# Four scatters of a half body, each waiting for the landing of the one before

## The chip, the cores and the metric

One core of a Trainium2 chip. The time is the device time of the kernel in microseconds, as a median of runs. The core has TensorE (PE), VectorE (DVE), ScalarE (ACT), GpSimd (POOL) and SyncE (SP), and 16 DMA engines that all of them share.

## What is computed

An embedding lookup with pooling: 512 examples, 32 features, each feature with a table of 12500 rows of 64 float32. For each example and feature up to 20 ids are given and a length; the rows of the first `length` ids are added.

```python
B, F, V, L, E = (512, 32, 12500, 20, 64)
emb = flat[ids + offs]                       # (B, F, L, E)
mask = (jnp.arange(L_) < lengths[..., None]).astype(emb.dtype)
pooled = jnp.einsum('bfle,bfl->bfe', emb, mask)
out = pooled.reshape(Bq, F_ * E_)
return jnp.nan_to_num(out)
```

## The kernel before

The 32 features are done in two ways side by side. M = 22 of them are *counted*: the kernel loads the whole table of a feature, builds one-hot matrices of the ids on VectorE (L740, L742), multiplies them on TensorE to counts (L515), lets ScalarE copy these to SBUF (L470), and multiplies the counts with the table (L525). Each feature is two halves of 256 examples, each half 7 chunks, so 14 stages per feature. VectorE reads the sums of a half at L778. TensorE's features run in a hardware loop, ScalarE's, VectorE's and SyncE's instructions are written out.

The other 10 features are *gathered*. They make 40 tiles of 128 bags (a bag is one example and feature). In the prologue the bags are sorted by their length through 40 scatters to DRAM (L402), so that bags of like length share a tile. Then GpSimd fetches, for tile after tile, the rows of slot l of all 128 bags with one indirect DMA (L427), as many slots as the longest bag of the tile has. `rows` has 8 buffers, one for each tile of a body; there are 5 bodies of 8 tiles. Gathers of one tile alternate between two semaphores, and each waits for the landing of the last one on its own semaphore. So about two are in flight.

VectorE adds the rows of a tile (L800, `add_rows`) at fixed places in its own program: tile t is added in stage ADDS of a feature, the first in feature 2, the last in feature 18, stage 4. It waits there for the tile's landed rows. SyncE fills the buffer with zeros and new row numbers when a tile was added. After every 4th tile VectorE cleans the 4 sums of the half body and signals `gathered_ready`. GpSimd then scatters the four sums, 64 float32 for each of 128 bags, to their places in the output (L437, `put`). All of these are issued from GpSimd's one queue, in the order of the program: in a body, the put of the first half of the body before stands ahead of tile 2, that of the second half ahead of tile 6 (`PUT_AT = 2`). The last two puts come behind all gathers.

The four scatters of a put share the semaphore `gathered_stored[x]` (x is the half). Who waits for it: VectorE ahead of the first sum of the same half one body later (L795), and GpSimd at the end. `fill_begun` is a counter that nobody waits for.

Of the kernel before, what the change touches and what calls it, by code (L numbers as in the profile page):

```python
# [36 lines left out]
SLOTS = BUFFERS // 2  # L37
PUT_AT = 2

def turn(l):  # L40
    return l % 2
# [40 lines left out]
def build_embedding_bag(nc, ids, lengths, tables, lookup_ids, lookup_lengths, lookup_place, ramps, triangle,  # L82
# [43 lines left out]
    with ExitStack() as ctx:  # L126
# [6 lines left out]
        def sem(name):  # L133
            return ctx.enter_context(nc.semaphore(name))
# [115 lines left out]
        fill_begun = sem("fill_begun")  # L250
        added = sem("added")
        gathered_ready = sem("gathered_ready")
        gathered_stored = [sem(f"gathered_stored{x}") for x in range(2)]
# [47 lines left out]
        def sorted_tile(t):  # L301

            return TILES - 1 - t // 2 if t % 2 == 0 else t // 2

        def column(t):
            return t % BUFFERS * BODIES + t // BUFFERS
# [76 lines left out]
        @block.gpsimd  # L383
        def _(pool):
            for out, pattern, base, by in (
                (value, [[1, L + 1]], 0, 0),
                (first_row, [[V, G], [0, L]], M * V, 0),
                (position, [[0, G], [1, L]], 0, 0),
                (records[:, :, L], [[P, TILES]], 0, 1),
                (lane[:], [[1, 1]], 0, 1),  # L390
            ) + tuple(
                (last_rank[:, column(k):column(k) + BODIES],
                 [[(sorted_tile(k + BUFFERS) - sorted_tile(k)) * P, BODIES]], sorted_tile(k) * P + P - 1, 0)
                for k in range(BUFFERS)
            ):
                nc.gpsimd.iota(out, pattern=pattern, base=base, channel_multiplier=by).then_inc(iotas_done, 1)
            last_row = pool.to_reg(F * V - 1)

            for k in range(BLOCKS):
                pool.wait_ge(records_ready, k + 1)  # L400
                for t in range(k * G, (k + 1) * G):
                    nc.gpsimd.indirect_dma_start(  # L402
                        out=sorted_records, out_offset=bass.IndirectOffsetOnAxis(ap=rank[:, t:t + 1], axis=0),
                        in_=records[:, t, :], in_offset=None).then_inc(records_out, 16)
            pool.wait_ge(records_out, 16 * TILES)
            for t in range(BUFFERS):
                s = sorted_tile(t)
                nc.gpsimd.dma_start(row_now[:, t, :], sorted_records[s * P:(s + 1) * P, :]).then_inc(first_records_in, 16)
            pool.wait_ge(depths_ready, 1)
            pool.wait_ge(first_records_in, 16 * BUFFERS)  # L410

            def gather(b, k):

                pool.wait_ge(buffer_ready[k], b * 32 + 16)
                pool.sem_inc(fill_begun, 1)
                n = pool.value_load(depth[0:1, bass.ds(b + column(k), 1)], min_val=2, max_val=L)
                landed = [pool.value_load(arrived[0:1, x, bass.ds(b + column(k), 1)], min_val=0, max_val=16 * L * BODIES)
                          for x in range(2)]
                with ExitStack() as deeper:
                    for l in range(L):  # L420
                        if l > 1:
                            deeper.enter_context(pool.If(n > l))
                        x = turn(l)
                        if l > 1:
                            pool.wait_ge(rows_in[k][x], landed[x] + 16 * sum(turn(i) == x for i in range(l)))
                            pool.sem_inc(fill_begun, 1)
                        nc.gpsimd.indirect_dma_start(  # L427
                            out=rows[:, k, l * E:(l + 1) * E], out_offset=None, in_=table_rows,
                            in_offset=bass.IndirectOffsetOnAxis(ap=row_now[:, k, l:l + 1], axis=0),
                            bounds_check=last_row, oob_is_err=False).then_inc(rows_in[k][x], 16)  # L430

            def put(b, x):

                pool.wait_ge(gathered_ready, b * 2 + (x + 1))
                pool.sem_inc(fill_begun, 1)
                for k in range(x * SLOTS, (x + 1) * SLOTS):
                    nc.gpsimd.indirect_dma_start(  # L437
                        out=out_gathered, out_offset=bass.IndirectOffsetOnAxis(ap=place_now[:, k:k + 1], axis=0),
                        in_=gathered[:, k * E:(k + 1) * E], in_offset=None).then_inc(gathered_stored[x], 16)

            def body(b, first):
                for k in range(BUFFERS):
                    if not first and k % SLOTS == PUT_AT:
                        put(b - 1, k // SLOTS)
                    gather(b, k)

            body(0, True)
            with pool.Fori(1, BODIES) as b:
                body(b, False)
            for x in range(2):  # L450
                put(BODIES - 1, x)
                pool.wait_ge(gathered_stored[x], 16 * SLOTS * BODIES)
# [447 lines left out]
```

## Time and profile before

| what | us |
|---|---|
| time, median of 3 runs | 1190.97 (1186.9 to 1194.51) |
| span of the profiled execution, first to last instruction | 1287.7 |
| TensorE busy in it | 1118.5 |
| VectorE busy | 992.5 |
| ScalarE busy | 827.6 |
| GpSimd busy | 547.5 |

The profiled execution was recorded by the hardware profiler and is another one than the three that were timed. Its span alone is 96.7 us longer than the median of those; its own time with what lies around the span is not given. Durations are read from it, and are compared with the timed runs where they differ.

### The profile page before, as it was taken

The numbers are of one execution on the slowest core, as the hardware profiler recorded it, in microseconds if no ns is written. First come the engines' busy times: TensorE is split into PE (matmuls) and PEld (weight loads), VectorE is DVE, ScalarE is ACT, GpSimd is POOL, SyncE is SP. The second block draws the span as 40 slices with busy tenths as digits, with TensorE's granted clock in tenths as the row PEclk, the third lists the DMA queues.
The fourth block names the chain that finished last, engine by engine and source line by source line (L and its number), as shares of the span: only waits on it lengthen the run. The fifth ranks groups of instructions, "written<-read, shape, count | busy, mean of one in ns | idle before, by whom it ended". The sixth has DMA issues, their size and how long they took to land.

```text
span 1287.7 us, 31751 instructions
## 1 busy us (share of the span) xinstructions
PE 1118.5 (87%) x10873; PEld 969.4 (75%) x10873; DVE 992.5 (77%) x2692; ACT 827.6 (64%) x1233; POOL 547.5 (43%) x519
## 2 busy tenths in 40 slices
PE   3379999896988878989979888979789999999996
PEld 1168888785876767778868767868678888888886
DVE  9657788884886867869868867969678898787881
ACT  4257787673756656757747566757557777787780
POOL 4865665556555455555565544555540101000000
PEclk9989999897999988999989989989989999999998
DMA  5324234241433333242414333242413213123120
GB/s 184 116 68 115 60 83 144 74 136 45 135 107 95 117 86 97 81 132 82 143 46 136 106 95 118 82 130 69 134 25 100 58 55 104 47 62 100 35 73 5
DMA packets 63916, 118.38 MB, mean 92 GB/s; under 512 B 30120, under 2 KB 31742, under 8 KB 63840
## 3 DMA queue, kind: packets, MB, share of 16 engines
q1 hardware_dynamic: 46608, 102.19, 25.5%
q0 software_dynamic: 16032, 15.00, 5.9%
q10 hardware_dynamic: 1200, 0.50, 0.2%
q14 instruction: 68, 0.56, 0.1%
q8 instruction: 8, 0.13, 0.0%
HBM read 87.19 MB, written 4.62 MB: 71 GB/s over the span
## 4 chain that ended last, share of the span: by engine, by line
PE 73%; DVE 10%; another core or an unknown queue 7%; ACT 7%; issue 3%; DVEq 0%; POOL 0%; POOLq 0%
PE sums L525 48%; PE pairs L515 19%; PE rest L543 6%; DVE onehot_j L742 3%; ACT counts L470 3%; ACT table L482 2%; DVE gathered L800 1%; DVE onehot_p L740 1%; ACT rest L478 1%; DVE table L751 1%; ACT table L486 0%; DVE table L759 0%; DVEq L796 0%; DVE is_nan L768 0%
## 5 line engine op out<-in xcount | busy, mean ns | idle before, releaser
L525 PE MATMUL sums<-table,counts 128*128 128x192 bf16 x8624 | 909.0, 251 | 0.8 <-issue 0.8
L470 ACT ACTIVATE counts<-pairs 128x588 int16<-128x588 f32 (+1 forms) x968 | 617.0, 650 | 368.9 <-PE pairs L515 262.7
L525 PEld LDWEIGHTS sums<-table,counts 128*128 128x128 fp8e3 x8624 | 776.3, 98 | 55.0 <-issue 0.4
L427 POOL DMA_INDIRECT rows<-tables,row_now x413 | 453.3, 1098 | 376.7 <-issue 206.1
L742 DVE TENSOR_SCALAR onehot_j<-ramp,j_of,worth 128x296 bf16<-128x296 f16 x1848 | 536.3, 353 | 0.0
L515 PE MATMUL pairs<-onehot_j,onehot_p 128*128 128x294 bf16 x1892 | 410.4, 297 | 112.8 <-ACT counts L470 67.3
L740 DVE TENSOR_TENSOR onehot_p<-ramp,p_of 128x768 bf16<-128x768 f16 x308 | 169.9, 552 | 253.7 <-PE pairs L515 172.9
L515 PEld LDWEIGHTS pairs<-onehot_j,onehot_p 128*128 128x128 bf16 x1892 | 178.2, 98 | 187.3 <-issue 107.8
L543 PE MATMUL rest<-table,minus_eye 128*128 128x448 bf16 x352 | 102.5, 373 | 38.2 <-ACT table L482 17.1
L486 ACT ACTIVATE table<-rest 128x896 f32<-128x896 f32 x88 | 80.8, 918 | 35.3 <-remote 23.6
L437 POOL DMA_INDIRECT out_gathered<-gathered,place_now x40 | 42.4, 1061 | 132.3 <-DVE gathered L771 121.0
L482 ACT ACTIVATE table<-rest 128x896 f32<-128x896 f32 x88 | 80.8, 918 | 26.1 <-remote 9.8
L800 DVE TENSOR_REDUCE gathered<-rows 128x64 f32<-128x1280 f32 x40 | 94.3, 2356 | 0.0
L478 ACT ACTIVATE rest<-table 128x896 f32<-128x896 f32 x88 | 80.7, 917 | 0.0
L751 DVE TENSOR_TENSOR table<-table 128x896 f32<-128x896 f32 x66 | 71.5, 1083 | 0.0
L759 DVE TENSOR_TENSOR table<-table 128x896 f32<-128x896 f32 x66 | 69.5, 1053 | 0.0
L543 PEld LDWEIGHTS rest<-table,minus_eye 128*128 128x128 bf16 x352 | 24.2, 98 | 58.4 <-ACT table L482 25.6
L402 POOL DMA_INDIRECT sorted_records<-records,rank x40 | 45.6, 1139 | 26.3 <-DVE records L617 14.4
L778 DVE TENSOR_REDUCE pooled<-sums 128x128 f32<-128x384 f32 x44 | 23.8, 542 | 21.3 <-PE sums L525 20.5
L728 DVE TENSOR_SCALAR onehot_j<-ramp,j_of,worth 128x296 bf16<-128x296 f16 x44 | 17.3, 392 | 0.0
L726 DVE TENSOR_SCALAR onehot_p<-ramp,p_of 128x128 bf16<-128x128 f16 x44 | 12.8, 291 | 0.0
L771 DVE COPY_PREDICATED pooled<-is_nan,zeros 128x256 f32<-128x256 uint8 x22 | 10.0, 453 | 0.8
(68 smaller groups left out, 79.8 us busy)
## 6 DMA issues: line engine op xcount, KB each, us to landing
table<-tables SPq DMA_DIRECT2D x154, 448.0 KB
rows<-zeros SPq DMA_DIRECT2D x40, 640.0 KB
rows<-tables,row_now POOLq DMA_INDIRECT x413
out_counted<-pooled SPq DMA_DIRECT2D x132, 21.0 KB
rows<-lookup_ids SPq DMA_DIRECT2D x1, 903.0 KB, 8.5
rows<-lookup_lengths SPq DMA_DIRECT2D x1, 903.0 KB, 10.2
out_counted<-pooled SPq DMA_DIRECT2D x44, 1.0 KB
sorted_records<-records,rank POOLq DMA_INDIRECT x40
```

The lines of the kernel that those rows point to most:

```text
L427: nc.gpsimd.indirect_dma_start(out=rows[:, k, l * E:(l + 1) * E], out_offset=None, in_=table_rows, in_offset=bass.IndirectOffsetOnAxis(ap= ...
L470: nc.scalar.activation(dst, src, ACT.Copy).then_inc(counts_saved, 1)
L478: nc.scalar.activation(rest[:, :, 0:CE // 2], both_halves(0, c), ACT.Copy).then_inc(chunk_copied, 1)
L482: nc.scalar.activation(both_halves(1, c), rest[:, :, 0:CE // 2], ACT.Copy).then_inc(middle_ready, 1)
L486: nc.scalar.activation(both_halves(2, c), rest[:, :, 0:CE // 2], ACT.Copy).then_inc(low_saved, 1)
L515: last = nc.tensor.matmul(pair(h, c, q)[:, x, 0:WIDE], onehot_p[:, s, k, :, side], onehot_j[:, s, i + 1, 0:WIDE], start=True, stop=True)
L525: last = nc.tensor.matmul(sums[h][:, k * PARTS * E:(k + 1) * PARTS * E], counts[h][:, j, :, k], parts[:, :, j, :, 1], start=(j == 0 and k ...
L543: last = nc.tensor.matmul(rest[:, x, 0:CE // 2], minus_eye[:], upper_halves(part)[:, half], start=False, stop=True, skip_group_check=True)
L740: nc.vector.tensor_tensor(onehot_p[:, s, 1:, :, :], ramp_twice.unsqueeze(1).to_broadcast([P, PAIRS, P, 2]), of_chunk.unsqueeze(2).to_broad ...
L742: nc.vector.tensor_scalar(onehot_j[:, s, i + 1, :], ramp[:, 2 * P:], j_of[:, n:n + 1], worth[:, 0:1], ALU.is_equal, ALU.mult).then_inc(one ...
L751: nc.vector.tensor_tensor(table[:, 1, sl], table[:, 0, sl], upper_halves(0)[:, sl], ALU.subtract).then_inc(rest_done, 1)
L800: nc.vector.tensor_reduce(out=gathered[:, k * E:(k + 1) * E], in_=rows[:, k, :].rearrange("p (l e) -> p e l", e=E), axis=AX_X, op=ALU.add)
```

## The change

In a put, GpSimd issued four scatters one behind the other. Now the second, third and fourth each wait until the one before has landed, that is, until `gathered_stored[x]` has counted its 16 increments, and each such wait is followed by one increment of `fill_begun`.

```diff
                 pool.wait_ge(gathered_ready, b * 2 + (x + 1))
                 pool.sem_inc(fill_begun, 1)
-                for k in range(x * SLOTS, (x + 1) * SLOTS):
+                for i in range(SLOTS):
+                    k = x * SLOTS + i
+                    if i:
+                        pool.wait_ge(gathered_stored[x], b * (16 * SLOTS) + 16 * i)
+                        pool.sem_inc(fill_begun, 1)
                     nc.gpsimd.indirect_dma_start(
                         out=out_gathered, out_offset=bass.IndirectOffsetOnAxis(ap=place_now[:, k:k + 1], axis=0),
                         in_=gathered[:, k * E:(k + 1) * E], in_offset=None).then_inc(gathered_stored[x], 16)
```

## Rows read from the trace of the kernel before

**Rows 1.** The page: span, and busy time of two engines.

```profile
span 1287.7 us, 31751 instructions
PE 1118.5 (87%) x10873; PEld 969.4 (75%) x10873; DVE 992.5 (77%) x2692; ACT 827.6 (64%) x1233; POOL 547.5 (43%) x519
```

**Rows 2.** The page: the chain that ended last, by engine and line.

```profile
PE 73%; DVE 10%; another core or an unknown queue 7%; ACT 7%; issue 3%; DVEq 0%; POOL 0%; POOLq 0%
PE sums L525 48%; PE pairs L515 19%; PE rest L543 6%; DVE onehot_j L742 3%; ACT counts L470 3%; ACT table L482 2%; DVE gathered L800 1%; DVE onehot_p L740 1%; ACT rest L478 1%; DVE table L751 1%; ACT table L486 0%; DVE table L759 0%; DVEq L796 0%; DVE is_nan L768 0%
```

**Rows 3.** Groups by line, GpSimd, 84 to 960 us: count, busy, mean, idle before.

```profile
L427 POOL DMA_INDIRECT rows<-tables,row_now x413 | 453.3, 1098 | 376.7 <-issue 206.1 <-DMA rows<-tables,row_now 170.7
L437 POOL DMA_INDIRECT out_gathered<-gathered,place_now x32 | 33.5, 1046 | 15.5 <-issue 9.5 <-DVE gathered L771 6.0
```

**Rows 4.** Timeline of GpSimd, the last gather: start, duration.

```profile
958.21 1.00 POOL L427 DMA_INDIRECT rows<-tables,row_now  x1 [0.51 <-issue]
```

**Rows 5.** VectorE's sums: the ninth and the last in the timeline.

```profile
369.37 2.30 DVE L800 TENSOR_REDUCE gathered<-rows 128x64 f32<-128x1280 f32 x1
...
1074.68 2.38 DVE L800 TENSOR_REDUCE gathered<-rows 128x64 f32<-128x1280 f32 x1
```

**Rows 6.** Timeline of VectorE: reading a feature's first half (features 0, 3, 16, 17, 21).

```profile
98.08 0.55 DVE L778 TENSOR_REDUCE pooled<-sums 128x128 f32<-128x384 f32 x1
...
252.87 0.55 DVE L778 TENSOR_REDUCE pooled<-sums 128x128 f32<-128x384 f32 x1
...
1017.02 0.54 DVE L778 TENSOR_REDUCE pooled<-sums 128x128 f32<-128x384 f32 x1
...
1066.62 0.54 DVE L778 TENSOR_REDUCE pooled<-sums 128x128 f32<-128x384 f32 x1
...
1260.40 0.56 DVE L778 TENSOR_REDUCE pooled<-sums 128x128 f32<-128x384 f32 x1 [4.06 <-PE sums L525]
```

**Rows 7.** Windows: length, busy PE, PEld, DVE, ACT, POOL, clock, DMA share, GB/s.

```profile
252.90:1017.00 764.10, 666.28 (x6456) 579.45 (x6454) 591.12 (x1571) 489.35 (x730) 391.68 (x362) 0.94 0.34 97
1066.60:1260.40 193.80, 190.88 (x1949) 169.86 (x1947) 154.45 (x447) 148.53 (x221) 4.97 (x4) 1.00 0.24 70
```

**Rows 8.** Windows within the first put and at the ninth.

```profile
297.00:299.00 2.00, 0.00 (x0) 0.00 (x0) 0.00 (x0) 0.00 (x0) 1.50 (x2) 1.00 0.05 17
299.00:301.00 2.00, 0.00 (x0) 0.00 (x0) 0.00 (x0) 0.00 (x0) 1.59 (x2) 0.67 0.09 33
...
1013.00:1019.00 6.00, 5.12 (x51) 4.35 (x51) 5.87 (x20) 2.35 (x4) 3.97 (x4) 1.00 0.06 22
```

**Rows 9.** Timeline of GpSimd around the first put: start, duration, idle before.

```profile
292.29 1.00 POOL L427 DMA_INDIRECT rows<-tables,row_now  x1 [1.98 <-issue]
...
294.89 1.03 POOL L437 DMA_INDIRECT out_gathered<-gathered,place_now  x1 [0.30 <-issue]
...
299.11 0.96 POOL L437 DMA_INDIRECT out_gathered<-gathered,place_now  x1 [0.30 <-issue]
300.37 1.03 POOL L427 DMA_INDIRECT rows<-tables,row_now  x1 [0.30 <-issue]
301.71 1.01 POOL L427 DMA_INDIRECT rows<-tables,row_now  x1 [0.30 <-issue]
303.76 0.99 POOL L427 DMA_INDIRECT rows<-tables,row_now  x1 [1.04 <-DMA rows<-tables,row_now]
```

**Rows 10.** Timeline of GpSimd, end of the prologue's scatters.

```profile
73.44 0.95 POOL L402 DMA_INDIRECT sorted_records<-records,rank  x1 [0.30 <-issue]
75.84 4.34 POOL L408 DMA_DIRECT2D row_now<-sorted_records  x8 [1.45 <-DMA sorted_records<-records,rank]
```

**Rows 11.** Timelines of VectorE and GpSimd where the ninth put begins.

```profile
1012.03 0.45 DVE L771 COPY_PREDICATED gathered<-is_nan,zeros 128x256 f32<-128x256 uint8 x1
...
1013.35 1.03 POOL L437 DMA_INDIRECT out_gathered<-gathered,place_now  x1 [54.13 <-DVE gathered L771]
```

**Rows 12.** Waits of VectorE: us in total, times, longest.

```profile
DVE onehot_p L740 <- remote: 70.4, 10, 12.1
```

## The prediction

> **What bounds the kernel now.** I read the page first, then the chain of waits, then the timelines of GpSimd (POOL in the rows) and VectorE (DVE), and last short windows around the scatters. TensorE (PE) is busy 1118.5 us of a span of 1287.7 [rows 1], and nearly three quarters of the chain that ended last is TensorE, 48% of it the product with the table and 19% the counting [rows 2]. GpSimd is not on that chain. So the body of the kernel is TensorE fed by VectorE, and the question is whether GpSimd, which the change makes slower, can get onto the chain.
>
> The reader should see two things about GpSimd. Its busy share is 43%, but between 84 and 960 us, while it gathers, it has no spare time worth the name: 413 gathers and 32 scatters are issued there, and of its idle time only 6.0 us is a wait for VectorE [rows 3]; the rest is issue time and landings of its own gathers. It is a serial chain of its own, 875 us long, and the 40 sums of VectorE hang on it in a fixed order. Second, in this execution it is well ahead: its last gather is issued at 958.21 [rows 4], the last sum starts at 1074.68 [rows 5].
>
> The execution with the recorder is not the one that is timed. Its span is 1287.7, the median of the runs is 1190.97, so at least 96.7 us of the span is not in a timed run, more by whatever lies around the span (no row gives that; I take 10 us, between 0 and 20). Where are they? From one feature's reading to the next it is 58.8 us in the stretch with gathers ((1017.02 - 252.87) / 13) and 48.5 us behind it ((1260.40 - 1066.62) / 4) [rows 6]. TensorE is idle 98 us in the first stretch and 3 in the second, and its work takes 666 / 13 = 51.3 us per feature against 191 / 4 = 47.7, since the clock granted is 0.94 against 1.00: it falls while the engine stands still [rows 7, 8]. Much of the idle time lies in freezes right behind the scatters: from 297 to 301 TensorE, VectorE and ScalarE do nothing at all while GpSimd issues on [rows 8]. If every feature took 48.5 us, the span would be 98 + 21 x 48.5 + 27 = 1144 (98.1 up to the first reading, 27.3 from the last one to the end); a timed run has some 1181 inside. So of the 134 us by which the 13 features exceed 13 x 48.5 at most 37 are left in a timed run, whatever their cause.
>
> **The change part by part.** It removes nothing and moves nothing. It adds 3 waits per half body, each for a scatter's landing, and 3 increments of a counter that nobody waits for (nothing). 10 half bodies, 30 waits.
>
> Cost of one wait. Before, scatters follow each other every 1.3 us: 294.89 to the gather behind the fourth at 300.37 is 5.48 for four with the second stretched, and the last steps are 1.26 [rows 9]; I take 1.28. After, the step is a scatter's landing and GpSimd's restart. The nearest rows: the last scatter of the prologue starts at 73.44, and what waits for its landing, a plain transfer, starts at 75.84: 2.40 us [rows 10], the lower bound. The gather at 303.76 waits for the landing of the one at 300.37: 3.39 us [rows 9], the upper bound. GpSimd's restart alone is seen where the put waits for VectorE: that ends at 1012.03 + 0.45 = 1012.48 and the scatter starts at 1013.35, 0.87 us later [rows 11]. I take 3.0, above the middle, because the follower in the gather's row is an instruction of the same kind. So each wait adds 3.0 - 1.28 = 1.7 us (1.1 to 2.1), three 5.1 (3.4 to 6.3).
>
> The Trainium skill (DMA: Bandwidth & Descriptors, Anatomy of one DMA — SWDGE (gpsimd) path) puts a fixed 2.0 us on such a transfer, most of it the receipt of the write; the row's 2.40 with a restart inside agrees with it. By the page's figure and the 0.87 of the trace the step would be 2.87, an estimate, and the cost for eight puts 45 us instead of the 48 below.
>
> What is queued behind the waiting instruction. The next tile's gather. In a plain tile the first gather starts 1.98 us after the previous one's end, because the sequencer loads three values from memory first; behind the four scatters the gap is 0.30, because the sequencer ran ahead under them [rows 9]. With waits it can run ahead under the last scatter only (about 1 us). I add 0.9 (0 to 1.7). Put together a put costs 6.0 us more (3.4 to 8.0). Eight puts lie before the last gather (32 scatters, [rows 3]), so the last gather comes 48 us later (27 to 64). The last two puts have no gather behind them, and end more than 190 us before the span does: free. If this cover were not there each would cost at most 6.
>
> Who waits. VectorE for the rows of each tile in order, then TensorE for VectorE's one-hots. VectorE also waits for four landed scatters before it overwrites the buffers a body later: the first put is issued at 294.89 and the sum that waits for it, the ninth, starts at 369.37 [rows 5, 9], so 8 us more hide there. SyncE refills a buffer behind a sum, not behind a scatter: nothing.
>
> Is there room for 48 us? In the recorded execution the last rows are landed at about 958.2 + 2.5 = 960.7 (3.39 less the restart of 0.87), against 1074.7: 114 us. In a timed run VectorE is earlier. From the last sum's start to the end are 213 us with hardly a stall [rows 5, 7]; 1191 - 10 - 213 = 968, and about 5 us of that tail may go too: 973. GpSimd without its 6.0 us wait lands at 954.7: 18 us. GpSimd itself may be faster without the recorder; no row tells, I allow 0 to 40 and take 18. Room: 36 us (3 to 68). 48 - 36 = 12, and rooms of the tiles before are 5 to 10 us larger, so only the last tiles are late. Against this stands that 36 is the middle of an uneven range: the room cannot be under 0, while the cost can reach 64. I put the wait of VectorE at 15 us, and nothing behind it is faster: every us by which a sum is late is handed on to TensorE, which has 213 us of fully busy work left. **1191 + 15 = 1206.** Against the profiled execution the sum is 1287.7 + 0: there the 114 us of room cover the 48.
>
> **The rivals.** (a) *The room covers it all*: GpSimd is 4% faster without the recorder, or the steps are 2.4 us. For it: the 114 us in the trace and that VectorE never waits for rows there. Against it: 97 us of the 114 are lent by freezes that a timed run lacks. Time: 1191.
>
> (b) *The other side, faster*: the freezes behind the scatters are caused by six indirect transfers issued back to back (four scatters, two gathers, [rows 9]) and are in part real. VectorE has 70.4 us in 10 waits that no released signal explains, up to 12.1 long [rows 12]. Spaced, the burst is gone. Speaks for it: the stretch with the freezes is the stretch with the puts, one of them just behind the first put; and the put at 1013.35, four scatters without gathers behind, leaves TensorE 5.12 of 6 us busy [rows 8], so it takes a longer burst. Against it: the 1144 above leaves at most 37 us for all stalls of a timed run; with two thirds of them at puts, 25 are to be had. If the spacing removes 25 and the room covers GpSimd, 1166. It decides for faster from 12 us real freeze on, provided the room holds; where both happen they cancel to about 1190 to 1195.
>
> The Trainium skill has a rule that bears on this (NOTIFIC — the notification-queue block, 7.1 Overflow: three behaviours, one of which stalls the engine): inside the block that writes trace records, a full pipeline holds the engine back rather than losing the record. By it the freezes belong to the recorder, the profile after would be shorter and the time would not, which is rival (a) with a prettier trace. No run here shows it; that the timed runs have no place for 134 us of slower features agrees.
>
> (c) *No room at all*: if GpSimd already bounds the timed run at the last tiles, the whole cost comes through: 1191 + 48 = 1239.
>
> **How the numbers follow.** No change can be told within 1% (12 us) here. Forecast, GpSimd late by 12 to 35 us: 0.40. (c): 0.08. (a), with lateness under 12 and with cancelling: 0.34. (b): 0.18. That the new wait passes at once is excluded: its count is the half body's own. Slower 0.48, same 0.34, faster 0.18. The range leaves out the fast end of (b) and all but the beginning of (c): 1174 to 1236. The forecast's own range is 1203 to 1226.
>
> **What the profile after would show.** Steps between the scatters of a put of about 3.0 us; a gap of 1 to 1.5 us before the gather behind them; the last gather at about 1000 if nothing else moves; no wait of VectorE for rows in the recorded run, as room is left there, or a short one if the freezes are gone, because then VectorE comes earlier. Freezes at the puts: still there if the recorder's load is the sum of the records, gone if it is the burst. I am wrong if GpSimd's pace without the recorder is more than 5% faster, or if the freezes are real.

## The result and the profile after

Slower, and by more than the range allowed: 1246.4 us median of 4 runs (1245.88 to 1248.3) against 1188.93 of 4 runs of before (1185.67 to 1194.51), ratio 1.048, 95% interval 1.045 to 1.051. That is 57.5 us more; the forecast was 15 more, the range ended at 1236. In the experiments, one run of the kernel before (1202.56 us, beside e5 to e8) was in the chip's slower state and is left out of the medians.

The page of the kernel after, with the busy line and the chain that ended last, its shares by engine and by line:

```profile
span 1244.4 us, 31793 instructions
...
PE 1094.2 (88%) x10873; PEld 960.8 (77%) x10873; DVE 990.7 (80%) x2692; ACT 828.7 (67%) x1233; POOL 544.7 (44%) x519
...
DMA 40%; issue 20%; PE 19%; POOL 6%; POOLq 6%; ACT 0%; DVE 0%; DVEq 0%
DMA rows<-tables,row_now 36%; PE sums L529 14%; POOL rows L427 6%; DMA out_gathered<-gathered,place_now 5%; PE pairs L519 4%; POOLq L417 3%; POOLq L416 1%; PE rest L547 1%; POOLq L422 1%; POOLq L425 0%; ACT table L486 0%; POOLq L426 0%; DVE gathered L804 0%; ACT counts L474 0%; POOL out_gathered L441 0%
```

Set this beside [rows 2]. The chain was 73% TensorE; now it is GpSimd's work from end to end: landings of its gathers, its issue time, and 5% landings of scatters. TensorE is on it for 19%, behind the last sums. This span and the time of the same execution, 1246.2, are 1.8 us apart, so the profile after is an ordinary execution, while that of before, 96.7 us longer than its timed runs, was not.

The timeline of GpSimd at the eighth put, after (start, duration, idle before and what ended it):

```profile
968.15 1.00 POOL L427 DMA_INDIRECT rows<-tables,row_now  x1 [0.30 <-issue]
969.45 1.03 POOL L441 DMA_INDIRECT out_gathered<-gathered,place_now  x1 [0.30 <-issue]
972.47 0.97 POOL L441 DMA_INDIRECT out_gathered<-gathered,place_now  x1 [1.99 <-DMA out_gathered<-gathered,place_now]
975.41 0.96 POOL L441 DMA_INDIRECT out_gathered<-gathered,place_now  x1 [1.97 <-DMA out_gathered<-gathered,place_now]
978.35 0.95 POOL L441 DMA_INDIRECT out_gathered<-gathered,place_now  x1 [1.98 <-DMA out_gathered<-gathered,place_now]
980.88 1.03 POOL L427 DMA_INDIRECT rows<-tables,row_now  x1 [1.58 <-issue]
```

The step between two scatters is 2.94 to 3.02 us, and the gather behind them starts 1.58 us after the last scatter's end where it was 0.30 [rows 9]. First scatter to next gather: 980.88 - 969.45 = 11.43 us. That is the cost as forecast. The last gather starts at 1018.87, where "about 1000" was foreseen. What was not forecast stands in the waits of the whole trace, after (us in total, times, longest), and in the view of the scatters' line:

```profile
PE pairs L519 <- DVE onehot_j L746: 105.0, 18, 26.0
DVE gathered L804 <- issue: 101.4, 6, 28.5
POOL out_gathered L441 <- DMA out_gathered<-gathered,place_now: 64.1, 30, 3.6
...
DVE gathered L804 <- DMA rows<-tables,row_now: 7.8, 1, 7.8
```

```profile
who waited for it (us, times):
  DVE gathered L804: 101.4, 6
  POOL out_gathered L441: 64.1, 30
busy tenths in 40 slices 0000000001001000000000000100100101000000
DMA to landing us min/median/max: 2.1/2.2/3.8
```

Six of VectorE's sums wait 101.4 us for the landing of a put, and one 7.8 us for rows. TensorE then waits 105 us for one-hots that VectorE had not made yet (63.2 us in e1, the kernel before profiled again). In the view of the group the wait is called "issue", since the semaphore was counted up over 1 us before the sum started (two values are loaded in between); the view of the scatters' line names who waited.

### The profile page after: what moved, and what is told of

It reads as the page before. It is cut to its first block, busy times and chain, and to the rows that moved or that the text cites. A ratio compares the mean times of both kernels' runs of the same rounds, so it can differ in the third digit from the quotient of the medians.

```text
span 1244.4 us, 31793 instructions
## 1 busy us (share of the span) xinstructions
PE 1094.2 (88%) x10873; PEld 960.8 (77%) x10873; DVE 990.7 (80%) x2692; ACT 828.7 (67%) x1233; POOL 544.7 (44%) x519
## 4 chain that ended last, share of the span: by engine, by line
DMA 40%; issue 20%; PE 19%; POOL 6%; POOLq 6%; ACT 0%; DVE 0%; DVEq 0%
DMA rows<-tables,row_now 36%; PE sums L529 14%; POOL rows L427 6%; DMA out_gathered<-gathered,place_now 5%; PE pairs L519 4%; POOLq L417 3%; POOLq L416 1%; PE rest L547 1%; POOLq L422 1%; POOLq L425 0%; ACT table L486 0%; POOLq L426 0%; DVE gathered L804 0%; ACT counts L474 0%; POOL out_gathered L441 0%
## 5 line engine op out<-in xcount | busy, mean ns | idle before, releaser
L529 PE MATMUL sums<-table,counts 128*128 128x192 bf16 x8624 | 898.7, 249 | 0.0
L529 PEld LDWEIGHTS sums<-table,counts 128*128 128x128 fp8e3 x8624 | 768.1, 97 | 52.7 <-issue 0.2
L519 PE MATMUL pairs<-onehot_j,onehot_p 128*128 128x294 bf16 x1892 | 405.0, 294 | 129.0 <-DVE onehot_j L746 105.0
L804 DVE TENSOR_REDUCE gathered<-rows 128x64 f32<-128x1280 f32 x40 | 93.9, 2349 | 109.1 <-issue 101.4
L441 POOL DMA_INDIRECT out_gathered<-gathered,place_now x40 | 39.5, 988 | 73.7 <-DMA out_gathered<-gathered,place_now 64.1
L402 POOL DMA_INDIRECT sorted_records<-records,rank x40 | 46.9, 1173 | 26.3 <-DVE records L621 14.4
L547 PEld LDWEIGHTS rest<-table,minus_eye 128*128 128x128 bf16 x352 | 24.9, 97 | 19.5 <-ACT table L486 7.5
```

The lines of the kernel that those rows point to most:

```text
L519: last = nc.tensor.matmul(pair(h, c, q)[:, x, 0:WIDE], onehot_p[:, s, k, :, side], onehot_j[:, s, i + 1, 0:WIDE], start=True, stop=True)
L529: last = nc.tensor.matmul(sums[h][:, k * PARTS * E:(k + 1) * PARTS * E], counts[h][:, j, :, k], parts[:, :, j, :, 1], start=(j == 0 and k ...
L547: last = nc.tensor.matmul(rest[:, x, 0:CE // 2], minus_eye[:], upper_halves(part)[:, half], start=False, stop=True, skip_group_check=True)
L804: nc.vector.tensor_reduce(out=gathered[:, k * E:(k + 1) * E], in_=rows[:, k, :].rearrange("p (l e) -> p e l", e=E), axis=AX_X, op=ALU.add)
```

## The experiments

All times are medians of one core's runs; ratios are to the kernel before, run beside each. That kernel's median was 1188.9 beside e1 to e4, 1189.4 beside e5 to e8 and 1193.9 beside e9 and e10.

**e1, the kernel before once more.** No edit.

> The unchanged kernel before, profiled once more. Theory A (GpSimd's chain sets the end already, through VectorE's wait for a put's landing ahead of the first sum of each half): the span comes out near the time of 1189, without the freezes, and VectorE shows waits ahead of its sums of tiles 16, 20, 24, 28, 32, 36, some 43 us together, released by scatters. Theory B (the kernel before has room, its freezes are real): the span is again near 1288 or, if shorter, VectorE shows no waits ahead of its sums.

1194.96 us in this one execution, span 1192.8, beside a median of 1188.92 (10 runs). The chain that ended last, by engine, from its page:

```profile
DMA 37%; PE 20%; issue 20%; POOL 8%; POOLq 6%; ACT 1%; DVE 0%; DVEq 0%
```

It is nearly the chain of the kernel after, and not the 73% TensorE of [rows 2]. Next the whole trace's wait of VectorE's sums, then GpSimd and VectorE at the eighth put, and a window at the first put (length, busy PE, PEld, DVE, ACT, POOL, clock, DMA share, GB/s):

```profile
DVE gathered L800 <- issue: 60.8, 6, 23.8
```

```profile
921.73 1.03 POOL L437 DMA_INDIRECT out_gathered<-gathered,place_now  x1 [0.30 <-issue]
923.06 0.97 POOL L437 DMA_INDIRECT out_gathered<-gathered,place_now  x1 [0.30 <-issue]
924.34 0.96 POOL L437 DMA_INDIRECT out_gathered<-gathered,place_now  x1 [0.30 <-issue]
925.60 0.96 POOL L437 DMA_INDIRECT out_gathered<-gathered,place_now  x1 [0.30 <-issue]
926.87 1.03 POOL L427 DMA_INDIRECT rows<-tables,row_now  x1 [0.31 <-issue]
```

```profile
929.09 2.29 DVE L800 TENSOR_REDUCE gathered<-rows 128x64 f32<-128x1280 f32 x1 [15.40 <-issue]
```

```profile
297.00:301.00 4.00, 3.96 (x43) 3.50 (x41) 3.15 (x11) 2.42 (x6) 3.08 (x4) 1.00 0.48 139
```

The kernel before is itself bound by GpSimd's chain: VectorE waits 60.8 us ahead of six sums, for puts. (That is more than the 43 expected. That VectorE makes up for part of each wait before the next one is likely, but no run here shows it.) In the execution of [rows 8] TensorE, VectorE and ScalarE stood still at the first put; here TensorE is busy 3.96 of 4 us through the same four scatters. The last scatter of the eighth put starts at 925.60, lands at about 927.8 (with the 2.2 us of the trace after), and the sum of tile 36 starts at 929.09. The same sum in the kernel after:

```profile
981.82 2.29 DVE L804 TENSOR_REDUCE gathered<-rows 128x64 f32<-128x1280 f32 x1 [20.86 <-issue]
```

It comes 52.7 us later, and from there to the end of the span both need the same: 1192.8 - 929.1 = 263.7 and 1244.4 - 981.8 = 262.6. The whole difference of the two executions, 51.6 us, lies ahead of that sum, and in both it starts 3.5 us behind the start of the put's last scatter.

**e2 and e3, one wait of the three.** In e2 only the second scatter waits (the edit below), in e3 only the fourth (`if i == 3`).

```diff
-                    if i:
+                    if i == 1:
```

> Only the second scatter of a put waits for the landing of the first; the third and fourth follow at once. One step of 2.97 us in place of 1.28, 8 puts up to the one that the sum of tile 36 waits for. Theory A: no room, 8 x 1.7 = 14 us more, 1203. Theory B (a room of some 36 us as I had it, and a cost of each wait that is larger than 1.7): within 3 us of before, 1189 to 1192.

> Only the fourth scatter of a put waits, for the landing of the first three. Step 2.97 in place of 1.28, and the sequencer can no longer run ahead under the scatters: the gap before the next gather is 1.57 in place of 0.30. Theory A: 8 x (1.7 + 1.25) = 24 us more, 1213. If the lost running ahead costs nothing: 1203, like the run with the wait at the second. Theory B: 1189 to 1195.

e2: 1203.96 us, ratio 1.012 (1.008 to 1.016). e3: 1216.78 us, ratio 1.023 (1.018 to 1.028). The sixth put, in e2 and then in e3, in the timeline of GpSimd:

```profile
756.56 1.00 POOL L441 DMA_INDIRECT out_gathered<-gathered,place_now  x1 [1.98 <-DMA out_gathered<-gathered,place_now]
757.86 0.95 POOL L441 DMA_INDIRECT out_gathered<-gathered,place_now  x1 [0.30 <-issue]
759.12 0.96 POOL L441 DMA_INDIRECT out_gathered<-gathered,place_now  x1 [0.30 <-issue]
760.38 1.03 POOL L427 DMA_INDIRECT rows<-tables,row_now  x1 [0.30 <-issue]
```

```profile
766.41 0.96 POOL L441 DMA_INDIRECT out_gathered<-gathered,place_now  x1 [1.97 <-DMA out_gathered<-gathered,place_now]
768.94 1.03 POOL L427 DMA_INDIRECT rows<-tables,row_now  x1 [1.57 <-issue]
```

One wait costs 15.0 us (9 to 18 by the interval), not nothing: there is no room to use up first. The same wait at the end of the put costs 12.8 us more than at its beginning. The gap before the next gather is 1.57 against 0.30, as if the sequencer could not prepare the gather under scatters that are still to be issued, and eight such gaps make 8 x 1.27 = 10. Both parts of a put's price reach the time.

**e4, the changed kernel with its puts earlier.**

```diff
-PUT_AT = 2
+PUT_AT = 0
```

> The changed kernel with its puts ahead of the first gather of each half (PUT_AT = 0 for 2), so that the sum which waits for a put no longer waits for two more tiles' gathers. GpSimd issues the same work. Theory A with VectorE's wait for the put as the link: what is left is the landing of the rows; from the trace after, rows are late by 87 us against an undisturbed VectorE where puts are late by 99, so 12 us less, 1234. Rival (the rows are the link, the put's place is nothing): no change, 1246.

1226.9 us, ratio 1.031 (1.025 to 1.036): 19.5 less than after, more than the 12 that I had worked out. The waits of VectorE's sums are now all for rows:

```profile
DVE gathered L804 <- DMA rows<-tables,row_now: 95.5, 12, 28.3
POOL out_gathered L441 <- DMA out_gathered<-gathered,place_now: 77.0, 30, 5.1
```

So the link was VectorE's wait for the put, and the next one behind it, 20 us away, is the landing of the rows.

**e5 and e6, the kernel before with its puts earlier.** The same edit to the kernel before; in e6 PUT_AT = 1.

> The kernel before with its puts ahead of the first gather of each half (PUT_AT = 0 for 2), no waits between scatters. Theory A (GpSimd's chain sets the end, through the put that the sum of tile 36 waits for): the link moves to the landing of the rows, which in the profiled run e1 are late by 30 us where the puts are late by 46, so 16 less, 1173; a little more if the puts now meet the refills, as the longer puts of e4 suggest. Rival (the place of the put is nothing without the waits): 1189.

> The same with PUT_AT = 1: the sum waits for one more tile's gathers in place of two or none. Of tiles 36 and 37 each takes some 18 us of GpSimd's time, so the put is earlier by as much as before at PUT_AT = 2. Theory A: rows are the link by then too, 1173 to 1178. Rival: 1189.

e5: 1171.93 us, ratio 0.983 (0.977 to 0.989). e6: 1175.69, ratio 0.985 (0.979 to 0.991). Against 1189.4 of before beside them (16 runs) that is 17.5 and 13.7 less, for an edit that only changes the order in GpSimd's queue. Waits of the sums in e5:

```profile
DVE gathered L800 <- DMA rows<-tables,row_now: 38.8, 6, 20.4
```

e4 less e5 is 55.0 us: the waits between the scatters cost about the same where VectorE doesn't wait for the put at all. In e6 the time came out as expected, but not wholly for the reason: I had expected the rows to be the link already, and four sums still wait for puts.

```profile
DVE gathered L800 <- issue: 30.8, 4, 20.5
DVE gathered L800 <- DMA rows<-tables,row_now: 16.9, 4, 13.2
```

**e7 and e9, VectorE's wait for the put taken away by a second buffer,** with the puts at their old place (PUT_AT = 2): e7 has the waits between the scatters, e9 the burst of before. The core of the edit:

```diff
-        gathered = sb("gathered", [P, BUFFERS * E], F32)
-        place_now = sb("place_now", [P, BUFFERS], I32)
+        gathered = sb("gathered", [P, 2 * BUFFERS * E], F32)
+        place_now = sb("place_now", [P, 2 * BUFFERS], I32)
...
-            with pool.Fori(1, BODIES) as b:
-                body(b, False)
+            with pool.Fori(0, (BODIES - 1) // 2) as j:
+                body(2 * j + 1, False, 1)
+                body(2 * j + 2, False, 0)
...
-                if b and k % SLOTS == 0:
-                    dve.wait_ge(gathered_stored[k // SLOTS], 16 * SLOTS * b)
+                n = b % 2 * BUFFERS + k
+                if b > 1 and k % SLOTS == 0:
+                    dve.wait_ge(gathered_stored[k // SLOTS], 16 * SLOTS * (b - 1))
```

> The changed kernel, its waits between scatters and its order of GpSimd's work kept, but with a second buffer for the sums and their places, so that VectorE waits for the put of a body earlier. This takes away the link alone. Theory A: only the landing of the rows is left, 12 us less than after, 1234; by the measured e4 (which also moved the puts and gained 19) down to 1227. Rival (the gain of e4 came of the puts' new place in the queue, not of VectorE's wait): 1246.

> The kernel before, four scatters in a burst at their old place, with the second buffer of e7. Theory A: VectorE no longer waits for puts, the landing of rows is the link, like e5: 1172. With e7 (1225) this gives the price of the waits alone on GpSimd's chain: 53 us, eight puts by 6.3 to 6.7. Rival (the waits cost through VectorE's buffer wait, and without it nothing): e7 and e9 would be within 10 us of each other, about 1215.

e7: 1225.39 us, ratio 1.028 (1.020 to 1.037). e9: 1167.31, ratio 0.978 (0.974 to 0.982), beside a before of 1193.89 (11 runs). Waits of VectorE in e7:

```profile
DVE gathered L806 <- DMA rows<-tables,row_now: 88.1, 13, 17.6
```

e7 gains what e4 gained (21.0 and 19.5), with the order of GpSimd's queue as it was. So the gain of e4 came of the wait, not of the new place. e7 less e9 is 58 us, or 63 when each is taken against the before beside it (36.0 above, 26.6 below). The price of the waits is a price on GpSimd's chain, whichever of the two links ties VectorE to it.

**e8, waits in the last two puts alone.**

```diff
-                    if i:
+                    if i and known(b, BODIES):
```

> Waits between the scatters only in the last two puts, which have no gather behind them. Theory A and the prediction both: free, 1189. Rival (the waits cost by what they do to the DMA queues or the clock, wherever they stand): a quarter of the change's cost, 1203.

1191.34 us, ratio 1.001 (0.998 to 1.005). The steps in those puts are 2.9 to 3.6 us and cost nothing, with no gather behind them. It is not the waiting as such. What the waits do to gathers beside them this run can't show, since none is left there.

**e10, the scatters singly between the gathers.** With the second buffer of e9, the scatter of slot k is issued behind the second gather of tile k, without any wait for another scatter.

```diff
                         bounds_check=last_row, oob_is_err=False).then_inc(rows_in[k][x], 16)
+                        if l == 1 and between:
+                            between()
...
-                    if not first and k % SLOTS == PUT_AT:
-                        put(b - 1, k // SLOTS, 1 - side)
-                    gather(b, k)
+                    gather(b, k, None if first else lambda: put_one(b - 1, k, 1 - side))
```

> With the second buffer, each scatter issued singly, behind the second gather of one tile each, where GpSimd otherwise stands idle for 1 to 2 us until the first gather has landed. Still one at a time, but the time between two scatters is filled with gathers and no wait is added. Theory A: the 5.1 us of a put's issue, and the burst's hold on the gathers, go out of GpSimd's chain for the most part, 8 x 3 to 4 us, 24 to 32 less than e9: 1143 to 1150; not under 1144 or so, where TensorE with 48.5 us per feature is the bound. Rival (GpSimd's idle time behind the second gather is not free, since the sequencer's own work fills it): within 5 us of e9.

1150.32 us, ratio 0.966 (0.961 to 0.970), 17.0 less than e9, against the 24 to 32 expected. One such scatter in the timeline of GpSimd, between its tile's second and third gather, and the waits of VectorE's sums:

```profile
605.11 1.00 POOL L427 DMA_INDIRECT rows<-tables,row_now  x1 [0.30 <-issue]
606.41 1.03 POOL L447 DMA_INDIRECT out_gathered<-gathered,place_now  x1 [0.30 <-DMA rows<-tables,row_now]
607.75 1.99 POOL L427 DMA_INDIRECT rows<-tables,row_now  x1 [0.31 <-DMA rows<-tables,row_now]
```

```profile
DVE gathered L811 <- DMA rows<-tables,row_now: 23.0, 5, 13.2
```

23 us of waits are left of 60.8. With some 1.8 us outside the span, 1150.3 is 4 to 5 us above the span of 1144 that I had worked out for a kernel whose features all take 48.5 us. It beats both kernels: 39 to 44 us under the kernel before, 96 under the changed one. A scatter that is issued where GpSimd would stand idle for a landing is cheap, but not free: over the 32 tiles the step from the second to the third gather adds up to 96.0 us, against 83.4 in e9, so 0.4 us a scatter. In a burst its step is 1.3 us, with a wait 3 us. The last gather starts 20.2 us earlier than in e9 (935.08 against 955.25), and not by the whole of what e9's eight puts take from first scatter to next gather, 45.4 us: the gathers at the scatters' old places have longer gaps before them again, 11.2 us for the eight against 2.4 in e9.

## Why the prediction was wrong

**The cost of a put was right.** Foreseen 3.0 us per step and 6.0 us per put; measured 2.94 to 3.02, and 11.43 against 5.14 (926.87 - 921.73 in e1), which is 6.3. Eight puts by 6.3 make 50 of the 57.5 us. Over the first eight puts the sums in the two traces are 95.8 and 42.7 us, a difference of 53; the early ones after the change took 11.8, 14.4 and 12.4. What lies outside the puts hardly differs: from the span's start to the eighth put it is 885.1 us after and 884.1 in e1. The rest, some 5 us, is within the spread of the runs of before (1182 to 1202), and e8, whose first eight puts have no waits either, took 877 us outside them. So whether the waits cost those few us too is open. My upper end, 64 us, held it. The two last puts were free, as foreseen (e8).

**The step that failed is the room.** "Is there room for 48 us?" came out at 36 us, and there is none (e2). Three things were wrong in it.

First, the wait that matters was dismissed by its first instance: "VectorE also waits for four landed scatters before it overwrites the buffers a body later: the first put is issued at 294.89 and the sum that waits for it, the ninth, starts at 369.37". That is the earliest of eight such pairs, and in e1 the first two do have some 17 us of room. From the third on, the sum starts 3.5 to 3.8 us behind the put's last scatter. I compared the rows of each tile with its sum; it was the put that had to be compared. The queue's order could be read in the code: body b issues the puts of body b - 1 ahead of its tiles 2 and 6, and tiles 0 and 4 need them. So the put that tile 36 waits for stands behind the gathers of tiles 36 and 37.

Second, a look at the later pairs would not have been enough, since the freezes had widened them: in the execution of the prediction they are 70 to 109 us apart, the first being the closest. The eighth put's last scatter, and the sum of tile 36:

```profile
921.94 0.96 POOL L437 DMA_INDIRECT out_gathered<-gathered,place_now  x1 [0.30 <-issue]
...
1022.58 2.38 DVE L800 TENSOR_REDUCE gathered<-rows 128x64 f32<-128x1280 f32 x1
```

Only with the freezes taken off does it show. Reckoned as for the rows, the sum belongs at 1191 - 10 - (1287.7 - 1022.6) + 5 = 920.9 in a timed run, and the put lets it start at 921.94 - 6.0 + 3.5 = 919.4 (3.5 is the step from the last scatter to the sum in e1): 1.5 us of room, where the rows gave 18.

Third, the room was filled up with an allowance of 18 us for a faster GpSimd that no row showed. In e1 GpSimd's last gather starts at 962.12, against 958.21 - 6.0 = 952.2: 10 us slower, not 18 faster. (The 10 us for what lies outside the span were too many, 1.7 to 2.2 was measured, but that error made the room smaller, not larger.) In e1 the sum of tile 36 starts 15.4 us late, behind its put, without any wait between scatters. The prediction had named two ways to be wrong, a GpSimd over 5% faster and real freezes; it was neither.

**The residual told it.** I had 1144 us for a kernel without stalls and some 1181 inside a timed run, and of the 37 us between them I wrote "at most 37 are left in a timed run, whatever their cause", at most a gain to be had. They were for the most part VectorE's lateness behind GpSimd: e9, without the wait for the put, is 22 to 27 us under the kernel before, and e10 39 to 44. With that reading the sum is 1191 + 48 = 1239, which stood there as rival (c) with 0.08; with the measured 6.3 per put it is 1241, against 1246. The chain of waits, not chance, made the loss, but (c) had been put as GpSimd bounding the last tiles; it bounds the kernel from the third put on.

**The rivals.** (a), the room covers it: out, by e2. (b), the freezes are real: out for the timed runs, and the spacing brought no gain. They were in the one execution of the prediction's rows; in the profiles of after and of e1 to e10 no wait is put down to an unknown releaser, and each span lies within 2.2 us of its own time; in the first profile [rows 12] have 70.4 us. What caused them in that execution was not found. The rule on the trace-writing block of the Trainium skill (NOTIFIC — the notification-queue block, 7.1) could explain them, but no run here shows it: eleven other executions with the recorder had none. Out of a single profile the freezes could not be told from a property of the kernel, except by the 97 us that the timed runs lack.

## What to carry to other kernels

If an engine issues a serial chain of DMAs, ask for each consumer which of the chain's entries is the last one it needs, in the order of the queue, and compare every such pair, not the first alone. Where the median is well above a floor worked out from stall-free stretches, as here by 37 us, look for a wait that somebody pays already; what lengthens its releaser then costs in full. If the profiled span is longer than the timed runs, profile the unchanged kernel again before room is read from it; failing that, take what it has too much off each pair.

A wait between DMAs that don't depend on each other turns issue time (1.3 us here) into landing plus restart (3.0 us), and ahead of what comes next the gap grows by 1.3 us more (e3 against e2). To issue them singly, put them where the engine stands idle anyway (0.4 us each in e10).

## What the runs showed of the hardware

Restart of GpSimd behind a landing: the scatter lands 2.2 us after its start in the median, the next one starts 2.94 to 3.02 us after it, so 0.8 us go by from the landing to the start. The Trainium skill (DMA: Bandwidth & Descriptors, Anatomy of one DMA — SWDGE (gpsimd) path) has 2.0 us fixed for such a transfer; the trace agrees within 0.2. The row of 2.40 us that the prediction set beside that figure is weaker support than it said: with the restart of 0.87 [rows 11] it leaves only 1.5 for the landing. The step measured here is within 0.15 of 2.0 + 0.87.

In e4 the three waits of a put are longer than after (77.0 us for 30 against 64.1, the longest 5.1), and a scatter lands 2.7 us after its start in the median, against 2.2. The put stands there close behind sums, whose buffers are being refilled. Whether the refills delay the scatters was not tried.
